# Expert loop of a GNN + mixture-of-experts layer: the up projection with its weights stationary

## The reference, cut to what matters

```
D_MODEL, EXPERT_DIM, NUM_EXPERTS, TOP_K = 256, 512, 8, 2
gate_logits = x_flat @ Wg + bg + bias
topk_vals, topk_idx = jax.lax.top_k(gate_logits, TOP_K)
topk_w = softmax(topk_vals)
h = relu(einsum('td,edh->teh', x_flat, W1) + b1)      # up projection
y = einsum('teh,ehd->ted', h, W2) + b2                # down projection
out = einsum('ted,te->td', y, combine)                # combine holds topk_w
x = x + out
```

## Time and profile before

| | |
|---|---|
| median of 3 runs | 1666.47 us (1665.78 to 1670.65) |
| profiled execution | 1666.33 us, span 1664.6 us, mean granted clock 0.932 |
| TensorE busy | 1444.7 us (87%) |
| weight loads | 808.6 us (49%) |
| VectorE busy | 705.1 us (42%) |
| ScalarE busy | 389.3 us (23%) |
| GpSimd busy | 165.3 us (10%) |

### The profile page before, as it was taken

How to read it: one execution, slowest core, us unless ns; L and a number is a source line. 1 busy time by engine, 2 the same in 40 slices (tenths; PEclk the granted TensorE clock), 3 DMA queues, 4 the chain that set the end, 5 groups by cost and what they waited for, 6 DMA issues and landing times.

```text
span 1664.6 us, 25197 instructions
## 1 busy us (share of the span) xinstructions
PE 1444.7 (87%) x8538; PEld 808.6 (49%) x8539; DVE 705.1 (42%) x1938; ACT 389.3 (23%) x1010; POOL 165.3 (10%) x145
## 2 busy tenths in 40 slices
PE   2565689889888999989999899989999863999996
PEld 2554444444443544445454444535444433666664
DVE  6989999999522220123001220122201356233332
ACT  1320444444302400032001310014000330333332
POOL 1000000000000000000000000000000004466663
PEclk9865799999999999989999999999999876999999
DMA  5153000000000000000000000000005090333333
GB/s 136 39 183 125 2 1 1 2 1 2 14 1 13 1 1 1 0 15 1 1 1 0 14 1 1 1 1 13 1 1 103 5 347 13 54 65 63 63 63 41
DMA packets 49551, 57.88 MB, mean 35 GB/s; under 512 B 14319, under 2 KB 41601, under 8 KB 49184
## 3 DMA queue, kind: packets, MB, share of 16 engines
q1 hardware_dynamic: 38688, 41.67, 8.7%
q0 software_dynamic: 10752, 14.69, 5.5%
HBM read 42.36 MB, written 13.99 MB: 34 GB/s over the span
## 4 chain that ended last, share of the span: by engine, by line
PE 79%; DVE 13%; issue 3%; DVEq 2%; ACT 1%; DMA 1%; POOL 1%; SPq 0%; POOLq 0%
PE bank L654 40%; PE bank L735 13%; PE bank L1148 6%; PE bank L1163 6%; PE bank L1752 3%; DVE ohS L1523 2%; PE bank L1697 2%; PE bank L1154 1%; PE bank L644 1%; DVE ohL L1409 1%; PE bank L738 1%; PE bank L1750 1%; PE bank L1140 1%; DVEq L505 1%; PE bank L1114 1%
## 5 line engine op out<-in xcount | busy, mean ns | idle before, releaser
L654 PE MATMUL bank<-at,m 125*128 125x500 fp8e4 (+1 forms) x3500 | 697.9, 356 | 10.4 <-issue 5.3
L654 PEld LDWEIGHTS bank<-at,m 125*128 125x128 f16 x3500 | 318.3, 98 | 342.8 <-issue 35.9
L663 DVE TENSOR_TENSOR aggT<-bank,dinvB 128x500 f32<-128x500 f32 (+1 forms) x70 | 42.3, 621 | 353.0 <-PE bank L654 352.8
L826 ACT ACTIVATE hT<-bank,prm 128x500 f32<-128x500 f32 (+1 forms) x70 | 40.5, 630 | 601.2 <-PE bank L738 601.2
L874 POOL TENSOR_TENSOR idJ<-idJ,wts 125x1400 f32<-125x1400 f32 x2 | 8.0, 4006 | 1380.6 <-DVE idJ L1032 1380.6
L788 DVE BATCH_NORM_STATS2 zst<-hT 128x6 f32<-128x500 f32 (+1 forms) x70 | 40.3, 617 | 198.4 <-ACT hT L826 198.4
L735 PE MATMUL bank<-hT,wcur 128*128 128x500 f32 (+1 forms) x280 | 124.2, 566 | 0.0
L1523 DVE TENSOR_SCALAR ohS<-iotaS,now 128x128 bf16<-128x128 bf16 x504 | 117.6, 306 | 0.0
L735 PE MATMUL bank<-aggT,wcur 128*128 128x500 f32 (+1 forms) x280 | 116.4, 538 | 0.0
L623 DVE SCALAR_TENSOR_TENSOR m<-bank,dinvP,m 125x256 f16<-125x256 f32 x100 | 48.0, 483 | 145.7 <-ACT m L635 145.7
L1148 PE MATMUL bank<-w1s,xtT 128*128 x224 | 107.7, 603 | 0.3 <-issue 0.2
(11 more groups left out here) (318 smaller groups left out, 1325.7 us busy)
## 6 DMA issues: line engine op xcount, KB each, us to landing
slrow<-sl_dram SPq DMA_DIRECT2D x26, 512.0 KB, 5.0
w1s<-in_L_ffn_W SPq DMA_DIRECT2D x1, 4096.0 KB, 14.5
w2s<-in_L_ffn_W SPq DMA_DIRECT2D x1, 4096.0 KB, 19.0
xin<-in_x SPq DMA_DIRECT2D x1, 2800.0 KB
x<-in_x SPq DMA_DIRECT2D x1, 2800.0 KB
out_rows<-x SPq DMA_DIRECT2D x1, 2800.0 KB
xn_dram<-xn SPq DMA_DIRECT2D x1, 2800.0 KB
wraw<-in_L_gnn_mlp_w SPq DMA_DIRECT2D x5, 512.0 KB, 3.7
```

What stands on the lines that cost most here:

```text
L654: last = pe.matmul(bank[banks[g % len(banks)]][:, 0:w], m[:, s, k, h * 128:(h + 1) * 128], at_block(g // H)[:, s, :], start=s == 0 and k = ...
```

## The change

The up projection swaps its operands: 128 columns of the expert's weights are stationary and the 128 turned rows move, four blocks of hidden channels by two halves of the input channels. The result has the hidden channels on the partitions at once and goes straight to `bank[4 + u]`, so that hidden (VectorE) and across (TensorE) are gone, with `h1` and their two semaphores. The stationary operand is no longer read from `w1s` at a register's address: VectorE copies the expert's weights of tile j+2, 1024 f32 on each partition, to one of two buffers `w1c` (in the region of `ohR`), once up(j) has left that buffer (`s_hT`). TensorE waits for that copy (`s_w1c`) instead of for the load of `w1s`, and no longer reads the expert for the up projection.

```diff
-        r = Region(after)
-        h1 = r("h1", [TT, 2, F], F32)
-        assert r.at <= hT_at
+        r = Region(ohR_at)
+        w1c = r("w1c", [128, 2, H, F], F32)
+        assert r.at <= after
...
-            def hidden(j, u):
-                dve.wait_ge(s_h1, j + 1)
-                dve.tensor_copy(h1[:, u, :], bank[2 + u][:, :]).then_inc(s_h1c, 1)
+            def staged(j, u, free):
+
+                e = dve.value_load(te[0:1, bass.ds(j, 1)], min_val=0, max_val=NE - 1)
+                if free is not None:
+                    dve.wait_ge(s_hT, free)
+                dve.tensor_copy(w1c[:, u, :, :].rearrange("p h f -> p (h f)"), w1s[:, bass.ds(e, 1), :, :].rearrange("p a h f -> p (a h f)")).then_inc(s_w1c, 1)
...
-                    if not (last and k == XB - 1):
-                        hidden(j + 1, (k + 1) % 2)
+                    if not (last and k >= XB - 2):
+                        staged(j + 2, k % 2, j + 1)
                     result(j, k % 2, k, None if first else XB * before + k + 2)
 
-            hidden(0, 0)
+            dve.wait_ge(s_w1, 16)
+            staged(0, 0, None)
+            staged(1, 1, None)
...
             def up(j, u):
 
-                e = pe.value_load(te[0:1, bass.ds(j, 1)], min_val=0, max_val=NE - 1)
                 pe.wait_ge(s_xtc, j + 1)
-                for h in range(H):
-                    last = pe.matmul(bank[2 + u][:, :], xtT[:, u, h, :], w1s[:, bass.ds(e, 1), h, :].rearrange("p a f -> p (a f)"), start=h == 0, stop=h == H - 1)
-                last.then_inc(s_h1, 1)
-
-            def across(j, u):
-                pe.wait_ge(s_h1c, j + 1)
+                pe.wait_ge(s_w1c, j + 1)
                 for k in range(FK):
-                    last = pe.transpose(bank[4 + u][:, k * TT:(k + 1) * TT], h1[:, u, k * 128:(k + 1) * 128], ident[:, :])
+                    for h in range(H):
+                        last = pe.matmul(bank[4 + u][:, k * TT:(k + 1) * TT], w1c[:, u, h, k * 128:(k + 1) * 128], xtT[:, u, h, :], start=h == 0, stop=h == H - 1)
                 last.then_inc(s_hT, 1)
...
                     down(j, u, None if first and k < 2 else j - 1)
-                    if not (last_group and k == XB - 1):
-                        across(j + 1, 1 - u)
```

More of the change, by code:

```diff
@@ L444, in gnn_ffn_program @@
         s_xtc = sem("s_xtc")
-        s_h1 = sem("s_h1")
-        s_h1c = sem("s_h1c")
+        s_w1c = sem("s_w1c")
         s_hT = sem("s_hT")
@@ L1132, in experts_pe @@
             pe.wait_ge(s_tab, 2)
-            pe.wait_ge(s_w1, 16)
             pe.wait_ge(s_w2, 16)
@@ L1181, in experts_pe @@
             up(0, 0)
-            across(0, 0)
             group(0, True, False)
```

## The result

The changed kernel takes 1642.53 us (median of 4 runs, 1640.42 to 1652.13) against 1667.43 (4 runs, 1665.78 to 1670.65): a ratio of 0.986, 95% interval 0.9818 to 0.9901. Run again on another chip, it gave 0.9882 (0.9853 to 0.9911). It is faster, by 1.2 to 1.4%; the forecast was 1644. The profiled execution took 1643.12 us, its span is 1641.4 and the mean granted clock 0.926. Runs of one kernel differ by several microseconds, so steps of 1 or 2 us are read in the traces, and where the clock changes they need more than one trace.

What follows compares the result with a forecast made beforehand. TensorE's own work was taken to bound the expert stage; -21.3 us over 54 tiles and -1.7 at the head made -23.0 on 1666.33, so 1643.3, rounded up to 1644 us, range 1639 to 1660.

Steps and rivals of the forecast that it cites:

- The bound: Expert stage: TensorE's own work sets the time, 4.104 us a tile, so what leaves its queue leaves the time.
- The pair: Up projection: one weight load plus matmul of 128 columns takes 0.11 us, 16 a tile, 1.76 us.
- Rival B: Up projection: a load and matmul pair costs 0.130 us, period 4.03, time 1661 us; chance 6%.
- Rival E: Up projection: no weight load hides behind matmuls, period 5.37, slower at about 1735 us; chance 2%.
- The head: Start of the expert stage, up(0) to down(0): no copy of h or turns between, 1.7 us gained.
- VectorE's copy: Staging copy of 1024 f32 inside SBUF on VectorE: 0.69 us, with 2.56 us of room, so free.
- rival D: Copy starts over 0.83 us after ytb, waits out the scatter, TensorE stands before up: slower, 1675 us; chance 6%.
- GpSimd: Gather and scatter cycle, next to be late: keeps pace with 3.71 us a tile, 0.51 to spare, cost taken as 0.
- rival C: GpSimd, held for VectorE's whole copy, becomes the bound: 3.89 us a tile, time 1659 us; chance 8%.
- the 0.81 of the estimate: Port between VectorE and GpSimd: by the skill's page GpSimd loses 0.81 us a tile, time 1664 us.
- The sum: Whole kernel: 21.3 us from the loop and 1.7 from the head, 23.0 us less than 1666.33.

## Why the prediction was right

**The bound** was right. TensorE is busy in all of 170.00 us after as before, and putting the turns back gives back 23.4 us of 23.8.

**The pair** was right in kind and 1.5 ns short: 0.1115 for 0.11, which is 54 x 16 x 0.0015 = 1.3 us and explains the whole of 20.0 gained in the loop instead of 21.3. The reason I gave, that load and matmul overlap, holds; which of the two sets the pace I had left open, and the run with 64 columns shows that the load does. Rival B's 0.130 falls: what it took for an uncovered rest in L1128's 112 columns is for the most part the load's own 0.11. Rival E falls with it, and with E the rule of the Trainium skill ("TensorE: Matmul & The Clock Gate", "The mechanism") as I had read it: no load here is for another row group, and they hide all the same, 0.1115 apart. The same section also lets a load go ahead into a background weight buffer, which my reading left out.

**The head** gave 2.7 us instead of 1.7, and the extra 1.0 is luck. I had the clock rise at the same moment as before, 1421.2; it rose about 1418.3, having fallen some 3 us earlier as well. The run with the turns put back has the same head, for its turns stand behind down(0). There the clock rose at 1421.3 (a mean of 0.85 over 1421 to 1422), and the head came out as forecast:

```profile
1417.06 5.65 PE bank L1152 x32
1422.71 0.22 PE bank L1143 x2
1422.92 1.73 PE bank L1161 x8
```

From up(0) to down(0) that is 5.86 us, 1.66 less than the 7.52 of before. The second profile of the changed kernel has 4.96, with the clock back 2.3 us into up(0). So the same code takes 4.9 or 5.9 us, by where the stretch at the lower clock lies. An up(0) without a pause isn't what brought the clock back early, since it had none in the run with the turns either, where the clock rose 4.2 us into it. That the clock is the price here is shown by the kernel kept at work (1.3 us less); what sets the moment at which it falls stays open.

**VectorE's copy** was right: 0.69, and TensorE never waits for it. From ytb's end to the copy it is mostly 0.4 to 0.75 us, but about 1.0 in every fourth tile (0.92 ahead of the copy at 1451.06), so rival D's condition, a start later than 0.83, was met there. Rival D falls all the same: copies start from 0.7 before to 0.2 after the scatter does, and those that meet a running scatter are not held up by it.

**GpSimd** was right in what it costs and wrong in how I read it. "VectorE gave way by 0.2 and GpSimd by nothing" came from gathers alone; scatters do give way, by up to 0.49 us, and 7.6 in sum (96.4 against the 88.8 of the run with the copy on ScalarE). So does a gather at times: the one at 1521.06 took 1.29 with a copy that started 0.48 after it, while no gather in the loop took over 1.1 before the change or with ScalarE's copies. The mechanism of rival C was there, and the Trainium skill's page ("SBUF — State Buffer", "SBUF: two separate sides") had named it. But its price was not: a scatter is held up when it starts inside the copy, and only to that copy's end, by 0.13 a tile on average and not by the 0.81 of the estimate. With 1.72 for 1.59, GpSimd's cycle is 3.33 on average, still under 3.73; its lag behind ytb at the boundaries grew and was made up again, and TensorE waited for gathered rows only at the first two tiles (5.2 us, from before the first matmul).

**The sum.** 20.0 + 2.7 = 22.7 against a forecast of 23.0: a loss of 1.3 in the loop and a gain of 1.0 by the clock met, and 0.6 came from ahead of the stage. That the total came within 0.3 is luck; with the head of the run with the turns it would have been 20.0 + 1.7 = 21.7, still 1.3 from the forecast.

## What to carry to other kernels

When an operand swap trades a transpose for more weight loads, look in the trace for the narrowest stream of load and matmul pairs of the same type: the distance between their starts is the price, not the duration that a load is shown with. Then look at what the engines beside it have left over in the new, shorter period, boundary by boundary, and not on average. A contention that shows up in a trace is worth removing only if the engine that it slows is on the path; here 7.6 us of it cost nothing. And before a step of 1 us at the start of a stage is explained, look where the granted clock changes in another trace of the same code.

## What the runs showed of the hardware

- A pair of f32 weight load and matmul, full array, took 0.111 to 0.112 us with 128 moving columns and with 64, and 0.058 with 64 moving columns and 64 columns of weights, at a granted clock of 1.00.
- A copy of 1024 f32 inside SBUF takes VectorE 0.69 us and ScalarE 1.06. VectorE's holds up a scatter of GpSimd that starts inside it, to the copy's end less some 0.13 us (2.03 for an end at 0.57, 1.83 for one at 0.38); a second copy right behind added nothing where it ended inside the scatter and 0.08 where it ran to the scatter's end, and ScalarE's copies held up none (1.587 on average).
- In the other direction, a copy that meets a gather 0.65 us after the gather's start took 0.87 instead of 0.69; a copy that starts inside a scatter took 0.69, and the scatter 1.59 (1450.96).
